# Splitting the negated score maxima on GpSimd instead of VectorE, in the two cross-attentions with 32 channels

## The reference

```python
x = x + _L0_xattn_ref(_layernorm(x, axis=-1), ctx_2048, ctx_2048)
# heads are blocks of 32 rows of d, for each batch element
scores = q^T k * 32 ** -0.5        # over the 32 channels of a head
weights = softmax(scores)
out = weights applied to v, heads put together again
```

## Time and profile before

| | |
|---|---|
| median of 3 runs | 1240.51 us (1238.07 to 1244.02) |
| profiled execution, span | 1239.3 us |
| around the span (profiled execution's own time less its span) | not listed; the median of the runs is 1.2 us above the span |
| mean granted clock of TensorE | 0.963 |
| TensorE busy | 1109.8 us (90%) |
| VectorE busy | 792.8 us (64%) |
| ScalarE busy | 573.5 us (46%) |
| GpSimd busy | 351.6 us (28%) |
| first cross-attention with 32 channels | 161 to 217.7 us |
| second | 364.8 to 420 us |

### The profile page before, as it was taken

One profiled execution on the slowest core, in us unless ns is written; L12 is line 12 of the kernel. 1 busy time (PEld: TensorE's weight loads), 2 busy tenths in 40 slices (PEclk: granted clock), 3 DMA queues, 4 the chain that ended last, 5 costly groups with the idle time before them and its releaser, 6 DMA issues. The chain is left out here.

```text
span 1239.3 us, 24482 instructions
## 1 busy us (share of the span) xinstructions
PE 1109.8 (90%) x9258; PEld 690.4 (56%) x9258; DVE 792.8 (64%) x2213; ACT 573.5 (46%) x1193; POOL 351.6 (28%) x416
## 2 busy tenths in 40 slices
PE   4888899796999979989999989999999979986898
PEld 2456644465775444455666645456777645662465
DVE  6833477758578544476888577575355476879855
ACT  3767424563334433445444445433533134548443
POOL 2544303100001400023555413215777113532000
PEclk9888899897989989999999999999999999996999
DMA  9000000000023021000000000145666400000001
GB/s 378 32 1 2 1 1 2 1 1 1 1 84 140 2 84 53 0 1 2 3 3 2 2 2 2 47 188 164 196 193 192 142 1 1 3 2 0 1 1 34
DMA packets 23491, 60.85 MB, mean 49 GB/s; under 512 B 3681, under 2 KB 12009, under 8 KB 22480
## 3 DMA queue, kind: packets, MB, share of 16 engines
q1 hardware_dynamic: 18864, 48.92, 11.4%
q0 software_dynamic: 4512, 10.37, 2.7%
HBM read 52.95 MB, written 8.29 MB: 49 GB/s over the span
## 5 line engine op out<-in xcount | busy, mean ns | idle before, releaser
L860 ACT ACTIVATE PT<-PS 128x384 f32<-128x384 f32 (+1 forms) x320 | 153.2, 531 | 184.3 <-PE PS L673 136.8
L793 DVE CUSTOM_DVE_ANT_0 junk<-PS,TRI 128x128 bf16<-128x128 f32 (+1 forms) x384 | 112.7, 353 | 3.9 <-PE PS L654 0.2
L269 PE MATMUL PS<-identb 128*128 128x512 bf16 x420 | 103.4, 385 | 6.4 <-PEq L626 1.8
L911 POOL TENSOR_TENSOR OD<-OD 128x256 f32<-128x256 f32 x24 | 17.4, 725 | 272.2 <-DVE OD L832 272.2
L654 PE MATMUL PS<-KS,QM 32*128 32x128 f32 (+1 forms) x768 | 86.8, 347 | 7.5 <-DVE QM L827 6.6
L901 POOL TENSOR_SCALAR_AFFINE_SELECT PT<-PT 128x512 f32<-128x512 f32 x96 | 61.0, 635 | 102.9 <-ACT PT L860 102.9
L832 DVE RECIPROCAL OD<-OD 128x256 f32<-128x256 f32 x40 | 69.9, 1747 | 30.9 <-ACT OD L868 25.9
L673 PE MATMUL PS<-QM,KS 32*128 32x256 f32 (+1 forms) x768 | 88.5, 348 | 0.0
L654 PEld LDWEIGHTS PS<-KS,QM 32*128 32x128 f32 x768 | 65.6, 184 | 30.2 <-DVE QM L827 16.6
L742 PE MATMUL PS<-PT,CST 128*32 128x256 f32 (+1 forms) x1280 | 75.4, 353 | 0.0
L1148 POOL TENSOR_TENSOR ROT<-RC,RS 128x512 f32<-128x512 f32 x16 | 20.3, 1269 | 175.0 <-DVE RS L1137 173.7
(11 more groups left out here) (374 smaller groups left out, 2612.4 us busy)
## 6 DMA issues: line engine op xcount, KB each, us to landing
WD<-w2d_in SPq DMA_DIRECT2D x47, 256.0 KB, 3.1
WU<-w2u_in SPq DMA_DIRECT2D x1, 5632.0 KB, 17.7
WA<-wl_in SPq DMA_DIRECT2D x1, 5137.0 KB, 15.5
GB<-gate_rows SPq DMA_DIRECT2D x8, 512.0 KB, 8.5
WU<-chosen SPq DMA_DIRECT2D x16, 256.0 KB, 5.9
WB<-wb_in SPq DMA_DIRECT2D x1, 3208.0 KB, 19.3
WA<-wa_in SPq DMA_DIRECT2D x1, 2560.0 KB, 15.4
WA<-w2s_in SPq DMA_DIRECT2D x6, 384.0 KB, 16.4
```

The lines of the kernel that those rows point to most:

```text
L269: pe.matmul(PS[:, bank, :].rearrange("p (a n) -> p a n", a=4), identb[:], identb[:].rearrange("p (a n) -> p a n", a=1).to_broadcast([P, 4, ...
L793: last = dve.tensor_tensor_reduce(junk[:, s, m * P:m * T + P], PS[:, s, m * T:m * T + (m + 1) * P], TRI[:, (1 - m) * P:T], 1.0, NEG, ALU.a ...
L860: act.activation(PT[:, g % 3, st_slot(k), 0:W], PS[:, st_bank(g, k), 0:W], ACT.Exp, scale=scale).then_inc(S["at_exp"], 1)
```

## The change

`parts` leaves VectorE's program and stands in GpSimd's, with the same five steps on the same tiles. GpSimd's loop now starts at g = -2 and has the split of quad g+2 at the head of each turn, ahead of the output step of quad g-3. The split waits for the maxima as before and, from the third quad on, for the transpose that read the same buffer of MX. VectorE's maxima wait, from the third quad on, for the split that read the same buffer of M4. Nothing changes for r > 1.

```diff
--- before.py
+++ after.py
@@ -796,24 +796,12 @@
                             last.then_inc(S["at_max"], 1)
                             return
                         if r == 1:
+                            if g >= 2:
+                                dve.wait_ge(S["at_parts"], d["at_parts"] + 5 * (g - 1))
                             mx = M4[:, g % 2].rearrange("p m s -> p s m")[:, 2 * half:2 * half + 2, :]
                         else:
                             mx = MX[:, g % 2].rearrange("p m (s c) -> p s m c", s=4)[:, 2 * half:2 * half + 2, :, spare(g)]
                         dve.tensor_reduce(mx, ps.rearrange("p s (m n) -> p s m n", m=2), AX, ALU.max).then_inc(S["at_max"], 1)
-
-                    def parts(g):
-
-                        col = lambda c: MX[:, g % 2].rearrange("p m (s c) -> p m s c", s=4)[:, :, :, c]
-                        steps = [lambda: dve.tensor_scalar(col(0), M4[:, g % 2], -1.0, None, ALU.mult),
-                                 lambda: dve.tensor_tensor(R4[:, g % 2], M4[:, g % 2], col(0), ALU.add),
-                                 lambda: dve.tensor_scalar(col(1), R4[:, g % 2], -1.0, None, ALU.mult),
-                                 lambda: dve.tensor_tensor(S4[:, g % 2], R4[:, g % 2], col(1), ALU.add),
-                                 lambda: dve.tensor_scalar(col(2), S4[:, g % 2], -1.0, None, ALU.mult)]
-                        dve.wait_ge(S["at_max"], d["at_max"] + 2 * g + 2)
-                        for n, step in enumerate(steps):
-                            if n:
-                                dve.wait_ge(S["at_parts"], d["at_parts"] + 5 * g + n)
-                            step().then_inc(S["at_parts"], 1)
 
                     def shift(g):
                         U, v = place(g)
@@ -842,8 +830,6 @@
                                 norm["apply"](dve, 2)
                             if norm is not None and g == -1:
                                 norm["apply"](dve, 3)
-                            if r == 1:
-                                parts(g + 2)
                         if g >= 2 and (g - 2) % r == r - 1:
                             invert((g - 2) // r)
                     if after is not None:
@@ -912,12 +898,32 @@
                         pool.wait_ge(S["at_added"], d["at_added"] + U + 1)
                         pool.tensor_tensor(dst, dst, o[:, 0:T], ALU.add).then_inc(S["at_out"], 1)
 
+                    def parts(g):
+
+                        col = lambda c: MX[:, g % 2].rearrange("p m (s c) -> p m s c", s=4)[:, :, :, c]
+                        steps = [lambda: pool.tensor_scalar(col(0), M4[:, g % 2], -1.0, None, ALU.mult),
+                                 lambda: pool.tensor_tensor(R4[:, g % 2], M4[:, g % 2], col(0), ALU.add),
+                                 lambda: pool.tensor_scalar(col(1), R4[:, g % 2], -1.0, None, ALU.mult),
+                                 lambda: pool.tensor_tensor(S4[:, g % 2], R4[:, g % 2], col(1), ALU.add),
+                                 lambda: pool.tensor_scalar(col(2), S4[:, g % 2], -1.0, None, ALU.mult)]
+                        if g >= 2:
+                            pool.wait_ge(S["at_turned"], d["at_turned"] + g - 1)
+                        pool.wait_ge(S["at_max"], d["at_max"] + 2 * g + 2)
+                        for n, step in enumerate(steps):
+                            if n:
+                                pool.wait_ge(S["at_parts"], d["at_parts"] + 5 * g + n)
+                            step().then_inc(S["at_parts"], 1)
+
                     if prepare is not None:
                         prepare(pool)
                     if r > 1:
                         stage_values(0)
                         stage_values(1)
-                    for g in range(NQ + 3):
+                    for g in range(-2, NQ + 3):
+                        if r == 1 and g + 2 < NQ:
+                            parts(g + 2)
+                        if g < 0:
+                            continue
                         if r > 1 and g >= 2 and (g - 2) % r == r - 1 and (g - 2) // r + 2 < UNITS:
                             stage_values((g - 2) // r + 2)
                         if g < NQ and causal:
```

## The result

The changed kernel takes 1276.69 us (median of 4 runs, 1275.52 to 1277.92) against 1242.26 us before (4 runs, 1238.07 to 1245.52): ratio 1.0272, 95% interval 1.0244 to 1.0300, so 34 us slower. The direction was forecast; the size was not: 14.2 us were forecast (1254.7, with a range of 1246 to 1265).

A forecast was written before the change was run, and what follows sets the result against it. Early rounds were taken as bound by TensorE and the split together, later ones by VectorE's sum of work. First stage +6.2 and second +8.1, together +14.2 on 1240.5, gave 1254.7 us; range 1246 to 1265.

The forecast's parts named there:

- P: Time from the end of a quad's second reduce to its transpose: from about 1.17 to 1.60 us.
- (a): First transpose of a stage: 1.1 us earlier in the first stage, 0.34 us later in the second.
- (f): Fifth transpose to the second half of scores: 1.22 us instead of 1.73, so -0.51 us.
- held round: Round where the split of quad 5, 6 or 7 precedes an output step: 7.30 us first stage, 7.45 second.
- rival C: TensorE's clock falls to 1.2 GHz in three rounds of each stage: +13.8 us, so 1268.5; chance 0.04.
- (c): Second to third transpose of a stage: 4.67 us instead of 4.22, so +0.45 us.
- (d): First of the two rounds after the third transpose: 5.22 us instead of 4.80, so +0.42 us.
- (e): Second of the two rounds after the third transpose: 5.22 us instead of 4.80, so +0.42 us.
- rival A: GpSimd's queue order does not hold ScalarE's copy: 1241.8 us, or 1236.1 with cheap steps; chance 0.12.
- Rival B: All five split steps on GpSimd cost the ceiling price, 0.43 us each: 1264.9 us; chance 0.08.

The follow-up runs named there:

- fill runs: The changed kernel with eight unread matmuls in TensorE's pauses before the products of quads 3, 4 and 5: ratio 1.0140 to the kernel before.

## Why the prediction was wrong

The steps in its own order, first stage, after against before. The steps of the chain are read from the timeline of the changed kernel:

| step | forecast | measured |
|---|---|---|
| five steps on GpSimd, first start to last end | 1.40 | 1.53 (192.91 to 194.44) |
| reduce's end to GpSimd | 0.09 | 0.15 |
| GpSimd to the transpose | 0.11 | 0.05 |
| P | 1.60 | 1.73 |
| (a) first transpose after the first reduce | -1.1 | -0.8 |
| (a) to (f), first reduce to the fourth round | -0.3 | +0.3 |
| a held round at full clock, first stage | 7.30 | 7.40 |
| a held round at full clock, second stage | 7.45 | 7.54 |
| both stages without the clock's share | +14.2 | +15.9 |
| the clock's share | 0 (rival C: +13.8) | +19.0 |

**Right:** the queue order as the cause, the buffer and the wait through which it acts, which quads, and the price. The steps lie inside the bounds that were set (0.29 and 0.34 us from start to start). The length of three held rounds was off by 0.3 us, the sum without the clock by 1.7, of which P has most: it is 0.13 too short and counts 14 times in the forecast's own sum, in (a), (c), (d), (e) and the three held rounds of each stage. Two slips of the working carry no weight: the first reduces end at 164.74 (162.38 + 2.36), not 164.72, and the terms of rival A's low price add up to 4.7 us, not 4.4.

**Wrong:** one step, rival C, and the 0.04 that it was given. The forecast had seen that TensorE would stand still for "about 2.5 of 7.3 us in three rounds of each stage", and dismissed the low clock on a single row, 2.18 us busy of 4.00 at a clock of 1.00. That row shows that one stretch with pauses kept its clock; it is no evidence for every such stretch. The same trace had other places that were not weighed: in a pause of 4.8 us, from 226.8 to 231.6, the clock fell to 0.50 (0.66 on average from 228 to 232). Nothing in it bounded the length between. The fill runs show the cause: the same holds with the pauses filled cost 19.0 us less.

The price of C was off as well, though less. It was worked out as half clock in the six held rounds, 13.8 us. The rounds have only 1.5 and 1.8 us of it (23.69 less 3 x 7.40, and 24.38, from 410.63 to 435.01, less 3 x 7.54). The larger part, 7.7 and 8.0 us, lies behind the last hold, where the forecast had said that "the rest of the stage is only moved". The clock fell at the last pause, and the work that follows took 17.1 us of the first stage and 20.5 of the second until it was back. The forecast with C was 1268.5, still 8 us short.

**Rival B's price.** It took all five steps at a high price. The two-input step on 128x8 takes 0.205 us on GpSimd, against 0.172 on VectorE, the one-input step 0.26 against 0.185. From start to start a step is 0.32 against 0.21, a factor of 1.5. On GpSimd most of a step is its fixed part: at the 2.1 ns an element that the forecast read from larger tiles, 8 elements are 0.02 of the 0.205 us.

The table in section 4.1 of the Trainium skill's page "GPSIMD Engine Reference", which rival B cited, has the factor of about 2 for two inputs alone, and puts one input at roughly the rate of VectorE. The trace agrees with neither on steps of this size: 1.2 and 1.4 by the durations above. The 2.1 us of rival B took the factor for all five steps, three of which have one input. By the page as it stands they would be 2 x 0.42 + 3 x 0.21 = 1.5 us, an estimate from its factor and VectorE's 0.21; 1.53 was measured, near it only because the steps with two inputs were cheaper than that (0.29) and those with one dearer (0.34).

**The two levels of the clock.** In the windows above the clock is 0.51 or 1.00 over long stretches. The Trainium skill's page "TensorE: Matmul & The Clock Gate" says in its Part 1 that the clock has two levels, 1.2 and 2.4 GHz, by how busy the engine has been; the trace agrees. The section "HAM oscillation" of that page of the Trainium skill says that idle gaps between bursts throttle the engine again. The fill runs agree with this, but the gaps that it describes, waits of 3 to 5 us for transfers, are longer than the 1.96 to 2.10 us here, two of which in six did not cost the clock.

## What to carry to other kernels

When a step moves to an idle engine, list everything in that engine's queue and who waits for it: here the step itself cost 3.3 us, its place in front of another step 12.6, and the clock that TensorE lost by the pauses 19.0. A pause on TensorE can be priced twice, once for its own length and once at half clock for the work behind it. Here four of six pauses of about 2 us had this second price, and the last one of each stage had most of it; ask first what runs behind the last pause. If a pause can't be avoided, unread matmuls ahead of the waiting instruction are worth a try: here they gave back all 19.0 us.

## What the runs showed of the hardware that was not expected

- At the last pause of about 2 us TensorE went to half clock for 17 us, though it was then busy for 16.45 of 17.26 us with shifted scores and products. With eight dense 128x512 matmuls put in, the clock was back within 0.1 us of their end, 3.6 us after their start (one run, both stages). Without them it came back in this stage behind 3.5 us of products alone; which work brings the clock back, and why the same kinds of matmuls did so within 4 us in the middle of the stage, is not shown.
- Pauses of the same length, in the same stage, kept the clock and lost it (1.96 us, the second and the third of the changed kernel's first stage).
- Pauses of 1.09 us kept the clock in one stage and pauses of 1.24 us lost it in the other, in the same run.
- On GpSimd a dependent step on 128x8 costs 0.29 us from start to start with two inputs and 0.34 with one; in the first split of the first stage one step took 0.35 instead of 0.20, while VectorE worked on layer norm (from 167.80). Steps beside VectorE's reciprocal (from 192.67) were as long as others.
- The kernel before took 1242 us beside the result and 1270 in the experiments, 2% apart, while the same stretch of a stage agreed to 0.03 us between the two; whether the chip or something else made the difference is not on record.
